# Clearing the sorted rows in sixteen parts behind the first stage's stores, with new engine orders

## The chip, the cores and the metric

The kernel runs on one core of one Trainium2 chip. The metric is the device time in microseconds of one execution, as the median of several runs. Lower is better.

## What is computed

The reference is a decoder of two layers on 64 sequences of 64 tokens of width 128, all in float32. Every sublayer is followed by a residual sum and a layer norm:

```
x = ln(x + retention(x))                 # layer 0: 8 heads, decay mask, group norm, gate
x = ln(x + cross_attention(ctx, x))      # 8 heads, masked, context of width 256
x = ln(x + moe(x))                       # 8 experts, top 2, merged by similarity, rerouted
x = ln(x + attention(x))                 # layer 1: 16 heads of 64, banded, softmax
x = ln(x + cross_attention(x, ctx))      # 16 heads of 8, over context and own tokens
x = ln(x + block(x))                     # attention, then 8 experts of width 512, top 2
```

The last sublayer's experts are sparse in the kernel: each token's row is copied to two places, sorted by expert, in a DRAM tensor `rows_x` of 38,912 rows of 132 floats. Rows of the sorted tensor to which no token goes must be zero, so `rows_x` is cleared before the first row is scattered into it. This clearing is what the change moves.

## The kernel before

**Tiling and stages.** The 64 sequences are 16 groups of 4 (256 tokens). Four slots (buffers and two PSUM banks each) hold four groups at a time, so there are four passes; group `4*n + s` is pass `n` in slot `s`. The program has four stages. Stage one (streams 0 to 15 of the orders, one for each group) does layer 0's sublayers: `first` is the retention, `second` the cross attention and all eight experts (steps `u0` to `u7` for the up products, `d0` to `d7` for the down products). Stage two (streams 16 to 31, for groups 0 to 15) does layer 1 up to the routing and scatters each token's row into `rows_x`. Stage three runs 39 tiles of 256 sorted rows through the wide experts, and stage four adds up and normalises.

**Between stages one and two** stands a small chain (`between`, steps `br`, `br.1`, `br.2` of stream 32): when the gate of all 16 groups is known, VectorE and TensorE work out which experts are merged and from which rows of `y_mid` each token's two results come (`first_rows`). GpSimd then gathers them (`fetch`, L1015).

**Orders.** Each engine is an in-order queue. What it issues next isn't decided at run time: for every stage and engine `ORDERS` holds a list of (stream, count) pairs, and `in_turn` advances the generator of that stream by so many steps. A step is what stands between two `yield`s, and it begins with the semaphore waits of its work. So a step whose input is late holds up everything behind it on that engine. A step is written here as stream:name, as 15:g for the gate of group 15.

**SyncE's queue (SP)** issues the plain DMAs. In stage one a stream's steps are `q` (the next pass's context and mask, four DMAs), `o2` (the next pass's x), `gb` (store of the state `x_mid`), `ye3` (store of four experts' results to `y_mid`), `u7` (the next pass's `XT`, L760) and `ye7` (the other four experts' results). Before this, SP issues the loads of the first pass, the weights `wb`, and then the clearing: it waits for a zeroed SBUF tile `blank` and issues four DMAs (L818), each of a quarter of `rows_x`. Nobody waits for them but GpSimd's first `fetch` of stage two:

```
if n == 0 and s == 0:
    pool.wait_ge(s_clear, 16 * (XROWS // 128 // BLANK))
```

The lines that the steps below touch: L1841 the projections of retention (`qk`, four matmul pairs), L1801 the 64-row scores, L1949 and L1828 an expert's up and down products, L1808 the turning of the state (`x`, `t1` to `t4`), L1938 the gate product of stage one (`g`), L1125 ScalarE's normalisation of the state (`on`), L2166 the gate product of stage two, L2171 the ranks (`rk`), L1707 the places on VectorE, L1081 the scatter into `rows_x`.

Of the kernel before, what the change touches and what calls it, by code (L numbers as in the profile page):

```python
# [30 lines left out]
SLOTS = 4  # L31
# [13 lines left out]
XROWS = 7 * CAP + 40 * NT  # L45
BLANK = XROWS // 128 // 4
# [77 lines left out]
def part_of(stage, i):  # L124
# [4 lines left out]
ORDERS = dict(sp1=(0, 1, 2, 1, 3, 1, 0, 1, 1, 3, 2, 1, 0, 4, 3, 1, 1, 3, 2, 2, 4, 2, 2, 1, 3, 1, 2, 1, 3, 3, 4, 4, 6, 1, 5, 2,  # L129
# [5 lines left out]
    pool1=(0, 4, 1, 2, 2, 2, 3, 2, 0, 1, 1, 2, 2, 1, 1, 1, 2, 1, 3, 2, 2, 1, 0, 2, 3, 1, 1, 2, 2, 2, 4, 2, 3, 1, 4, 2,  # L135
# [292 lines left out]
def build(nc, d, out, groups):  # L428
    passes = groups // SLOTS
    ctx = ExitStack()  # L430
    with ctx:
# [63 lines left out]
        blank = sb("blank", [128, 4 * WIDE])  # L495
# [252 lines left out]
        def _(sp):  # L748
# [26 lines left out]
            def loads(n, s):  # L775
                load_xT(n, s)
                load_context(n, s)
                load_x(n, s)

            def first(n, s):  # L780
                yield from ()

# [145 lines left out]
        def _(pool):  # L928
# [78 lines left out]
            def fetch(n, s):  # L1007
                if n == 0 and s == 0:
                    pool.wait_ge(s_clear, 16 * (XROWS // 128 // BLANK))
# [1300 lines left out]
```

## Time and profile before

| what | us |
|---|---|
| median of 3 runs | 1558.77 (1558.26 to 1558.95) |
| the profiled execution | 1557.2 |
| its span, first to last instruction | 1555.4 |
| TensorE busy in the span | 1366.5 (88%) |
| VectorE, ScalarE, GpSimd busy | 1109.8, 935.6, 671.9 |

The profile is of one execution. The span is 1.8 us under that execution's own time, and the median of the runs is 1.6 us over it. TensorE is the busiest engine. Its busy time is no floor by itself: it counts matmuls at the clock that was granted at the time, and the share differs from stage to stage. Stage one ends at about 480 us, stage two at about 1320, stage three at about 1490.

### The profile page before, as it was taken

What the parts mean: (1) busy time and instruction counts of PE and PEld (TensorE: products, weight loads), DVE (VectorE), ACT (ScalarE), POOL (GpSimd) and SP (SyncE); (2) the same over time, 40 slices, a digit from 0 to 9 for tenths busy, and PEclk for the clock granted to TensorE, in tenths of its full rate; (3) what the DMA queues carried; (4) which work ended last, traced back from release to release, by engine and by line L of the source; (5) the groups of instructions that cost most, each with busy time, mean ns of one, the idle gap of its engine ahead of it and who ended that gap; (6) DMA issues with size and microseconds to landing.
All of it is one profiled execution on the core that took longest, in us unless ns stands there. A gap on an engine that the chain in (4) does not pass through costs nothing.

```text
span 1555.4 us, 47442 instructions
## 1 busy us (share of the span) xinstructions
PE 1366.5 (88%) x19262; PEld 1123.0 (72%) x19262; DVE 1109.8 (71%) x3476; ACT 935.6 (60%) x2469; POOL 671.9 (43%) x1048
## 2 busy tenths in 40 slices
PE   5899999999988998899998899998899984999951
PEld 4688888888876777676776677776777763888851
DVE  3777787887876758888667887778876775445556
ACT  2555665655544687855878658795568962545412
POOL 5514433533316214655234753337441344254455
PEclk8899999999999999999999999999999996999985
DMA  9952122121022000110000110011100003676851
GB/s 333 384 174 83 35 83 92 53 65 66 15 74 74 9 12 18 44 30 29 10 21 25 36 43 10 14 32 37 29 23 9 13 23 100 208 224 211 237 148 42
DMA packets 112155, 123.21 MB, mean 79 GB/s; under 512 B 21984, under 2 KB 85216, under 8 KB 111680
## 3 DMA queue, kind: packets, MB, share of 16 engines
q1 hardware_dynamic: 105344, 106.53, 21.7%
q0 software_dynamic: 6592, 13.64, 2.8%
q8 instruction: 152, 2.49, 0.7%
q14 instruction: 67, 0.55, 0.1%
HBM read 64.99 MB, written 55.15 MB: 77 GB/s over the span
## 4 chain that ended last, share of the span: by engine, by line
PE 48%; DVE 23%; POOL 8%; ACT 8%; issue 6%; DMA 5%; SPq 2%; DVEq 0%; POOLq 0%; ACTq 0%
PE bank L1949 6%; PE bank L1816 5%; PE bank L1801 3%; PE bank L1828 3%; DMA Q<-in_wm 2%; PE bank L2036 2%; PE bank L2071 2%; PE bank L1997 2%; DVE P L1581 2%; DVE gs L1580 2%; ACT P L1226 2%; PE bank L1993 2%; PE bank L2203 2%; PE bank L2196 2%; POOL rows_x L1081 2%
## 5 line engine op out<-in xcount | busy, mean ns | idle before, releaser
L1816 PE MATMUL bank<-const,P 128*128 128x128 f32 x1152 | 167.9, 280 | 9.9 <-ACT P L1226 4.1
L1816 PEld LDWEIGHTS bank<-const,P 128*128 128x128 f32 x1152 | 129.8, 142 | 39.4 <-ACT P L1226 10.0
L1226 ACT ACTIVATE P<-bank,gs 128x128 f32<-128x128 f32 x512 | 141.3, 393 | 26.4 <-DVE gs L1570 25.9
L1949 PE MATMUL bank<-XT,wb 128*128 128x256 f32 x512 | 140.4, 398 | 7.0 <-ACT PT L1131 3.8
L1036 POOL TENSOR_TENSOR P<-P,gs 128x512 f32<-128x512 f32 x64 | 66.5, 1047 | 157.1 <-DVE gs L1617 156.7
L1234 ACT ACTIVATE PT<-bank 128x512 f32<-128x512 f32 x192 | 108.2, 614 | 28.9 <-PE bank L1816 28.6
L1091 POOL DMA_INDIRECT y_rows<-R,gidx x78 | 74.7, 958 | 92.5 <-DVE R L1756 73.7
L1570 DVE TENSOR_REDUCE gs<-bank 128x4 f32<-128x512 f32 x128 | 82.1, 682 | 39.4 <-PE bank L2071 38.8
L1949 PEld LDWEIGHTS bank<-XT,wb 128*128 128x128 f32 x512 | 89.3, 192 | 22.2 <-ACT PT L1131 7.5
L1580 DVE TENSOR_REDUCE gs<-bank 128x8 f32<-128x512 f32 x128 | 87.1, 681 | 24.5 <-PE bank L2009 12.1
L1198 ACT ACTIVATE P<-bank 128x256 f32<-128x256 f32 x128 | 48.5, 380 | 84.5 <-PE bank L1949 83.8
L1327 ACT ACTIVATE PT<-bank,Q 128x256 f32<-128x256 f32 x156 | 64.8, 475 | 56.5 <-PE bank L2196 55.7
L946 POOL TENSOR_SCALAR rstd<-mv 128x2 f32<-128x2 f32 x80 | 18.1, 226 | 183.1 <-DVE mv L1358 182.3
L1219 ACT ACTIVATE P<-P 128x512 f32<-128x512 f32 x128 | 80.3, 643 | 19.7 <-DVE P L1581 19.3
L1581 DVE TENSOR_TENSOR P<-bank,gs 128x512 f32<-128x512 f32 x128 | 88.5, 691 | 4.4
L1081 POOL DMA_INDIRECT rows_x<-XW,places x64 | 64.4, 1006 | 49.4 <-DVE places L1707 39.3
L2196 PE MATMUL bank<-XT,Q 128*128 128x256 f32 x312 | 77.1, 385 | 4.8 <-DMA Q<-in_wm 4.8
L1828 PEld LDWEIGHTS bank<-wb,P 128*128 128x128 f32 x512 | 73.5, 193 | 9.7 <-DVE P L1511 4.6
L1828 PE MATMUL bank<-wb,P 128*128 128x128 f32 x512 | 78.4, 280 | 2.3 <-DVE P L1511 2.2
L1015 POOL DMA_INDIRECT Q<-y_mid,first_rows x64 | 64.3, 1004 | 29.5 <-DVE first_rows L1556 16.6
L2203 PE MATMUL bank<-Q,PT 128*128 128x128 f32 x624 | 76.1, 275 | 0.0
L2203 PEld LDWEIGHTS bank<-Q,PT 128*128 128x128 f32 x624 | 74.8, 192 | 1.5
(298 smaller groups left out, 3723.3 us busy)
## 6 DMA issues: line engine op xcount, KB each, us to landing
Q<-in_wm SPq DMA_DIRECT2D x39, 578.5 KB, 4.2
rows_x<-blank SPq DMA_DIRECT2D x4, 5016.0 KB, 37.7
y_mid<-PT SPq DMA_DIRECT2D x16, 512.0 KB, 3.1
y_mid<-D SPq DMA_DIRECT2D x16, 512.0 KB, 3.0
XW<-rows_x SPq DMA_DIRECT2D x39, 132.0 KB, 2.5
wb<-in_wb SPq DMA_DIRECT2D x1, 4228.0 KB, 15.0
V<-in_ctxT SPq DMA_DIRECT2D x32, 128.0 KB, 3.4
XT<-in_xT SPq DMA_DIRECT2D x16, 128.0 KB, 2.2
```

The source lines that it names most:

```text
L1081: pool.indirect_dma_start(d["rows_x"][:, :], bass.IndirectOffsetOnAxis(ap=places[:, (n * SLOTS + s) * T + t, k:k + 1], axis=0), XW[s][:, t ...
L1219: act.activation(P[s][:, i, :], P[s][:, i, :], ACT.Exp, scale=scale).then_inc(p.of(s), 1)
L1226: ins = act.activation(P[s][:, i, 128 * g:128 * g + 128], banks[s][i][:, 128 * g:128 * g + 128], ACT.Exp, bias=gs[s][:, 0, 4 * i + g:4 * i ...
L1234: act.activation(dst[:, i, :], banks[s][i][:, :], ACT.Copy).then_inc(pT.of(s), 1)
L1570: dve.tensor_reduce(gs[s][:, 0, 4 * i:4 * i + 4], banks[s][i][:, :].rearrange("p (g m) -> p g m", m=128), AX.X, ALU.min).then_inc(b_s_sub. ...
L1580: st2(dve.tensor_reduce(mx, v, AX.X, most))
L1581: dve.tensor_tensor(P[s][:, i, :].rearrange("p (g m) -> p g m", m=width), v, each(mx, width), ALU.subtract).then_inc(s_sub.of(s), 1)
L1816: last = pe.transpose(tile(banks[s][i], t), tile(P[s][:, i, :], t), ident)
L1828: last = mm(tile(half(s, i + 1), t), tile(P4[s][:, i + 1, :], t), tile(B("down"), e), start=True, stop=True)
L1949: mm(half(s, 2 * (e % 2) + k), tile(B("gu"), 2 * e + k), XT[s][:, :], start=True, stop=True).then_inc(a_up_ps.of(s), 1)
L2196: mm(half(s, c), tile(part(wm[s], WM, "w1"), c), XT[s][:, :], start=True, stop=True).then_inc(m_up_ps.of(s), 1)
L2203: ins = mm(tile(half(s, 0), t), tile(PT4[s][:, c, :], t), tile(part(wm[s], WM, "w2"), c), start=c == 0, stop=c == NC - 1)
```

## The change

The four clearing DMAs ahead of the first stage are gone. In their place stands `clear_rows(k)`, which clears 4 or 5 of the 76 blocks of four rows that each partition holds, called once for each group directly behind its `gb` store. The first call waits for `blank`. GpSimd's `fetch` waits for all 16 parts. Nothing else in the code is changed; but the orders of stages one, two and three are written anew for all five queues. Stage four's are the same.

```
-BLANK = XROWS // 128 // 4
...
+            def clear_rows(k):
+                fours = XROWS // 128 // 4
+                lo, hi = fours * k // groups, fours * (k + 1) // groups
+                sp.dma_start(d["rows_x"].rearrange("(p a r) d -> p a (r d)", p=128, r=4)[:, lo:hi, :],
+                             over(blank[:, :], hi - lo)).then_inc(s_clear, 16)
...
                 sp.wait_ge(a_x.of(s), a_x.at(n, s, use=1))
                 sp.dma_start(token_rows(x_mid, n, s), X1[s][:, :, :]).then_inc(stored[s], 16)
+                if n == 0 and s == 0:
+                    sp.wait_ge(s_blank, 1)
+                clear_rows(n * SLOTS + s)
                 yield "ye3"
...
             sp.dma_start(wb[:, :], d["wb"]).then_inc(s_wb, 16)
-            sp.wait_ge(s_blank, 1)
-            each_row = XROWS // 128
-            for at in range(0, each_row, BLANK):
-                sp.dma_start(d["rows_x"].rearrange("(p a r) d -> p a (r d)", p=128, r=4)[:, at // 4:(at + BLANK) // 4, :],
-                             over(blank[:, :], BLANK // 4)).then_inc(s_clear, 16)
...
-                    pool.wait_ge(s_clear, 16 * (XROWS // 128 // BLANK))
+                    pool.wait_ge(s_clear, 16 * groups)
```

How far the orders moved, counted after writing every list out step by step. A step's move is the difference of its positions in the two lists.

```
queue, stage        steps   mean move
SP, one and two       148        1.4
GpSimd, one and two   448        1.2
ScalarE, one and two 1504        0.5
VectorE, one and two 1219        0.3
TensorE, one and two 2146        0.6
SP, three              78        1.4
GpSimd, three          39        1.1
ScalarE, three        195        1.7
VectorE, three         78        1.4
TensorE, three        273        2.4
```

The places of the lists that the prediction speaks of, written out (b before, a after):

```
SP, start      b  0:q 2:q 3:q 0:o2 1:q 1:o2 1:gb 2:o2 0:gb 0:ye3 0:u7 0:ye7 3:o2 1:ye3 1:u7 1:ye7 2:gb 2:ye3 4:q 4:o2 2:u7 3:gb 2:ye7 3:ye3 3:u7
               a  2:q 3:q 0:q 0:o2 0:gb 0:ye3 2:o2 0:u7 0:ye7 1:q 1:o2 1:gb 1:ye3 1:u7 1:ye7 3:o2 2:gb 2:ye3 2:u7 3:gb 4:q 2:ye7 3:ye3 3:u7
SP, end of one b  12:gb 12:ye3 15:gb 12:ye7 13:gb 13:ye3 16:ls 13:ye7 17:ls 14:gb 14:ye3 14:ye7 18:ls 15:ye3 15:ye7 19:ls
               a  12:gb 12:ye3 13:gb 14:gb 14:ye3 15:gb 12:ye7 16:ls 14:ye7 13:ye3 13:ye7 18:ls 17:ls 15:ye3 15:ye7 19:ls
TensorE, start b  0:qk 0:qk.1 0:qk.2 0:qk.3 0:vg 2:qk 0:st 0:y 0:y.1 3:qk 3:qk.1 3:qk.2 3:qk.3 2:qk.1
               a  0:qk 0:qk.1 0:qk.2 0:qk.3 0:vg 1:qk 0:st 1:qk.1 0:y 0:y.1 2:qk 1:qk.2 1:qk.3 3:qk
TensorE, 1->2  b  14:u5.1 14:d4 13:u7.1 14:u6 14:u6.1 14:d5 14:u7 14:u7.1 15:x 14:d6 15:g 15:u0 15:u0.1 15:u1 15:u1.1 13:d6 13:d7 br
               a  14:u5.1 14:d4 13:u7 13:u7.1 15:x 14:u6 14:u6.1 14:d5 15:g 14:u7 14:u7.1 15:u0 15:u0.1 15:u1 15:u1.1 14:d6 14:d7 br
ScalarE, 1->2  b  14:u4 14:d3 14:u5 14:d4 13:u7 14:u6 14:d5 15:on 14:u7 15:x 15:u0 15:g
               a  14:d3 13:u6 13:d5 12:d7 15:on 14:u5 14:d4 13:u7 15:x 14:u6 14:d5 14:u7 15:u0 15:g
TensorE, 2->3  b  30:t4 30:g 30:rk 31:t4 31:g 31:rk
               a  30:t4 30:g 31:t4 30:rk 31:g 31:rk
VectorE, 2->3  b  30:g 30:gb 30:rk 31:g 31:gb 31:rk
               a  30:g 30:gb 31:g 30:rk 31:gb 31:rk
```

## Rows read from the trace of the kernel before

**Rows 1.** Page, section 1: busy time of each engine

```profile
PE 1366.5 (88%) x19262; PEld 1123.0 (72%) x19262; DVE 1109.8 (71%) x3476; ACT 935.6 (60%) x2469; POOL 671.9 (43%) x1048
```

**Rows 2.** Windows: PE, PEld, DVE, ACT, POOL busy, PE clock, DMA share, GB/s

```profile
18.60:64.30 45.70, 36.41 (x525) 29.92 (x524) 29.18 (x72) 19.73 (x50) 29.95 (x35) 0.87 1.03 382
...
88.00:450.00 362.00, 348.77 (x3929) 302.98 (x3928) 286.06 (x892) 214.79 (x571) 134.16 (x206) 1.00 0.20 62
...
700.00:1000.00 300.00, 279.10 (x4886) 218.09 (x4885) 231.05 (x621) 215.12 (x569) 132.34 (x211) 1.00 0.09 24
```

**Rows 3.** Waits of PE on a DMA, 0 to 88 us, then 88 to 450

```profile
PE bank L1841 <- DMA XT<-in_xT: 3.2, 1, 3.2
...
PE bank L1841 <- DMA XT<-in_xT: 2.1, 1, 2.1
```

**Rows 4.** Timeline of SP, 18 to 90 us: start, duration, line, tensors

```profile
18.25 45.99 SPq L818 DMA_DIRECT2D rows_x<-blank  x4
64.34 14.65 SPq L768 DMA_DIRECT2D V<-in_ctxT  x2
...
87.38 0.81 SPq L768 DMA_DIRECT2D V<-in_ctxT  x2
```

**Rows 5.** Page, section 6: the clearing's DMAs, KB each, us to landing

```profile
rows_x<-blank SPq DMA_DIRECT2D x4, 5016.0 KB, 37.7
```

**Rows 6.** L760 of slot 1 at 6.87 us; timeline 16 to 21 us

```profile
DMA to landing us min/median/max: 8.1/8.1/8.1
...
16.70 0.42 DVE L1436 SCALAR_TENSOR_TENSOR Q<-Q,bank 128x256 f32<-128x256 f32 x1 [3.82 <-ACT Q L1152]
...
17.49 1.22 PE L1841 MATMUL bank<-XT,wa 128*128 128x256 f32 x2 [3.23 <-DMA XT<-in_xT]
...
18.64 1.99 PE L1801 MATMUL bank<-D,PT 64*64 64x128 f32 x32
```

**Rows 7.** Timeline of SP and PE, 135 to 151 us

```profile
143.59 0.82 SPq L768 DMA_DIRECT2D V<-in_ctxT  x2
...
146.22 1.47 SPq L760 DMA_DIRECT2D XT<-in_xT  x1
...
135.86 1.99 PE L1949 MATMUL bank<-XT,wb 128*128 128x256 f32 x8
...
150.29 1.62 PE L1841 MATMUL bank<-XT,wa 128*128 128x256 f32 x6 [2.15 <-DMA XT<-in_xT]
```

**Rows 8.** Timeline at the end of stage one, 447 to 465 us

```profile
447.45 0.22 POOL L956 TENSOR_SCALAR shift<-shift 128x2 f32<-128x2 f32 x1
...
450.30 0.86 ACT L1125 ACTIVATE XW<-R,shift,rstd 128x128 f32<-128x128 f32 x2
...
452.33 0.61 PE L1938 MATMUL bank<-wa,XT 128*128 128x8 f32 x4
...
464.31 1.22 POOL L1015 DMA_INDIRECT Q<-y_mid,first_rows  x1 [16.64 <-DVE first_rows L1556]
```

**Rows 9.** Timeline at the end of stage two, 1305 to 1314 us

```profile
1305.32 0.58 PE L2171 MATMUL bank<-gs,const 128*128 128x16 f32 x2 [3.52 <-DVE base L1423]
...
1307.02 0.17 DVE L1707 CAST places<-small 128x4 uint32<-128x4 f32 x1
1307.30 1.02 PE L2166 MATMUL bank<-wb,XT 128*128 128x8 f32 x4 [0.47 <-ACT XT L1213]
...
1309.46 0.33 DVE L1389 TENSOR_TENSOR small<-gs 128x2 f32<-128x2 f32 x1
...
1311.39 0.95 POOL L1081 DMA_INDIRECT rows_x<-XW,places  x1 [0.30 <-issue]
...
1313.79 0.95 POOL L1081 DMA_INDIRECT rows_x<-XW,places  x1 [1.45 <-DVE places L1707]
```

**Rows 10.** Windows, as rows 2, in the first 24 us

```profile
20.00:24.00 4.00, 3.20 (x46) 2.65 (x42) 1.86 (x4) 0.00 (x0) 0.00 (x0) 0.50 1.02 385
```

**Rows 11.** Waits, 1320 to 1490 us: us in total, times, longest

```profile
DVE small L1740 <- DMA Q<-in_wm: 24.5, 13, 6.4
```

More of the change, by code:

```diff
@@ L126, in part_of @@
     return f"{stage}.{i}" if i else stage
-ORDERS = dict(sp1=(0, 1, 2, 1, 3, 1, 0, 1, 1, 3, 2, 1, 0, 4, 3, 1, 1, 3, 2, 2, 4, 2, 2, 1, 3, 1, 2, 1, 3, 3, 4, 4, 6, 1, 5, 2,
[5 rows of a table removed]
-    pool1=(0, 4, 1, 2, 2, 2, 3, 2, 0, 1, 1, 2, 2, 1, 1, 1, 2, 1, 3, 2, 2, 1, 0, 2, 3, 1, 1, 2, 2, 2, 4, 2, 3, 1, 4, 2,
[14 rows of a table removed]
-    act1=(0, 4, 1, 3, 0, 1, 2, 3, 3, 3, 1, 1, 0, 3, 2, 1, 0, 1, 1, 2, 3, 1, 0, 1, 1, 1, 0, 2, 2, 1, 0, 1, 1, 2, 0, 1,
[58 rows of a table removed]
-    dve1=(0, 7, 2, 2, 3, 2, 0, 1, 1, 2, 0, 1, 1, 1, 0, 1, 1, 2, 2, 1, 1, 1, 3, 1, 1, 1, 2, 2, 3, 2, 1, 1, 0, 1, 2, 1,
[52 rows of a table removed]
-    pe1=(0, 5, 2, 1, 0, 3, 3, 4, 2, 4, 1, 4, 3, 1, 1, 1, 0, 2, 1, 3, 2, 1, 3, 1, 0, 1, 2, 2, 3, 1, 0, 1, 1, 2, 0, 1,
[79 rows of a table removed]
-    sp3=(1, 1, 3, 2, 1, 1, 5, 1, 2, 1, 0, 2, 4, 1, 7, 1, 2, 1, 6, 1, 4, 1, 5, 1, 6, 1, 7, 1, 8, 2, 11, 1, 9, 2, 10, 2,
[3 rows of a table removed]
-    pool3=(1, 1, 0, 1, 2, 1, 4, 1, 3, 1, 7, 1, 5, 1, 6, 1, 11, 1, 8, 1, 10, 1, 9, 1, 13, 1, 12, 1, 15, 1, 16, 1, 14,
-         1, 18, 1, 17, 1, 20, 1, 21, 1, 19, 1, 23, 1, 22, 1, 24, 1, 25, 1, 27, 1, 26, 1, 30, 1, 28, 1, 29, 1, 33, 1,
-         31, 1, 32, 1, 34, 1, 35, 1, 36, 1, 37, 1, 38, 1),
-    act3=(0, 1, 1, 1, 2, 1, 0, 4, 3, 1, 1, 4, 2, 3, 5, 1, 2, 1, 3, 4, 4, 3, 6, 1, 4, 2, 5, 4, 7, 1, 6, 2, 7, 1, 6, 2,
[5 rows of a table removed]
-    dve3=(3, 1, 2, 1, 0, 1, 1, 1, 0, 1, 1, 1, 2, 1, 3, 1, 6, 1, 4, 2, 7, 1, 5, 2, 6, 1, 8, 1, 9, 1, 7, 1, 10, 1, 11,
[4 rows of a table removed]
-    pe3=(0, 1, 2, 1, 1, 1, 0, 2, 3, 1, 0, 1, 1, 1, 0, 1, 1, 3, 0, 2, 2, 2, 1, 2, 2, 2, 4, 1, 5, 1, 3, 4, 2, 2, 4, 4,
[9 rows of a table removed]
@@ new lines @@
+ORDERS = dict(sp1=(2, 1, 3, 1, 0, 4, 2, 1, 0, 2, 1, 6, 3, 1, 2, 3, 3, 1, 4, 1, 2, 1, 3, 3, 5, 1, 4, 5, 6, 2, 5, 3, 7, 1, 5, 2,
[5 rows of a table added]
+    pool1=(0, 4, 1, 2, 2, 2, 3, 2, 0, 1, 1, 2, 2, 1, 1, 1, 2, 1, 3, 2, 1, 1, 2, 1, 0, 2, 2, 1, 3, 1, 1, 1, 3, 1, 2, 1,
[15 rows of a table added]
+    act1=(0, 4, 1, 3, 0, 1, 2, 3, 3, 3, 1, 1, 0, 3, 2, 1, 0, 1, 1, 2, 3, 1, 0, 1, 1, 1, 0, 2, 2, 1, 0, 1, 1, 2, 0, 1,
[57 rows of a table added]
+    dve1=(0, 7, 3, 2, 0, 1, 1, 2, 2, 2, 0, 1, 1, 1, 0, 1, 1, 2, 2, 1, 1, 1, 3, 1, 1, 1, 2, 1, 3, 2, 2, 1, 1, 1, 0, 1,
[53 rows of a table added]
+    pe1=(0, 5, 1, 1, 0, 1, 1, 1, 0, 2, 2, 1, 1, 2, 3, 5, 2, 3, 1, 1, 2, 1, 0, 2, 1, 3, 2, 1, 3, 1, 2, 1, 0, 1, 2, 1,
[79 rows of a table added]
+    sp3=(3, 2, 2, 1, 7, 1, 1, 2, 2, 1, 6, 1, 0, 2, 4, 1, 5, 1, 4, 1, 5, 1, 6, 1, 7, 1, 8, 2, 9, 2, 10, 2, 11, 2, 12,
[3 rows of a table added]
+    pool3=(0, 1, 1, 1, 3, 1, 2, 1, 5, 1, 4, 1, 7, 1, 6, 1, 8, 1, 9, 1, 10, 1, 11, 1, 13, 1, 14, 1, 12, 1, 16, 1, 15,
+         1, 17, 1, 18, 1, 21, 1, 19, 1, 20, 1, 24, 1, 22, 1, 23, 1, 27, 1, 26, 1, 25, 1, 28, 1, 30, 1, 29, 1, 31, 1,
+         33, 1, 32, 1, 34, 1, 36, 1, 35, 1, 37, 1, 38, 1),
+    act3=(0, 1, 1, 1, 0, 4, 1, 3, 3, 1, 1, 1, 3, 1, 2, 5, 5, 1, 4, 1, 3, 3, 4, 4, 5, 2, 7, 1, 5, 2, 6, 5, 8, 1, 7, 4,
[5 rows of a table added]
+    dve3=(0, 1, 1, 1, 2, 1, 3, 1, 0, 1, 1, 1, 2, 1, 5, 1, 3, 1, 4, 2, 5, 1, 8, 1, 6, 2, 7, 2, 10, 1, 11, 1, 8, 1, 9,
[3 rows of a table added]
+    pe3=(0, 1, 1, 1, 2, 1, 3, 1, 0, 4, 1, 4, 0, 2, 3, 2, 4, 1, 1, 2, 2, 4, 5, 1, 3, 2, 2, 2, 3, 2, 6, 1, 4, 3, 7, 1,
[9 rows of a table added]
```

458 rows, old and new, of tables (ORDERS, act1, act3, dve1) are left out of this document.

## Prediction

> **What bounds the kernel now.** I read the page first. TensorE is busy for 1366.5 of the span's 1555.4 us [rows 1], so time is won where TensorE stands idle, and lost where it is made to wait. The windows show where that is [rows 2]. While the four clearing DMAs drain, 18.6 to 64.3 us, the DMA engines are full (share 1.03, 382 GB/s) and TensorE is busy for 36.41 of 45.70 us. From 88 to 450 us, the rest of stage one, DMA has a share of 0.20 and TensorE is busy for 348.77 of 362 us: 13.2 us of idle time in all. In stage two a stretch of 300 us has 279.10 busy, so 20.9 idle.
>
> It is tempting to read the full DMA and the idle TensorE of the first 88 us as cause and effect. The list of waits doesn't bear it out: up to 88 us TensorE waits for a DMA once, 3.2 us, and from 88 to 450 us once again, 2.1 us [rows 3]. The first of these ends at 17.49 [rows 6], before the first clearing DMA is issued at 18.25 [rows 4]. The rest of the idle time in the ramp is the latency of four groups going through a chain of small steps on all engines, with no expert products yet to fill the gaps.
>
> What the clearing does hold is SP. Its four issues last 45.99 us, and the first context load behind them another 14.65 [rows 4]. That load is for pass two, which starts after 100 us. So the clearing is nearly free before the change, and taking it away from there wins by itself nearly nothing. What is left is what the new orders do, and whether the parts hurt where they now stand.
>
> **The clearing, removed at the start: 0.** SP is free from 18.7 us instead of from 79. But its next steps wait for their own inputs: the context of slot 3 is issued at 87.38 us, when its buffer falls free [rows 4], long after the clearing's issues. No engine waits for an earlier SP step. Bounds: 0 above; below, the clock rival under "rivals".
>
> **The sixteen parts: 0, at most 10.** The total is the same: 4 x 5016 KB [rows 5] is 20.5 MB, one part 1.28 MB on average, and at 382 GB/s [rows 2] 3.4 us of all DMA engines. The window from 88 to 450 us has 80% of DMA time unused, 290 us, for 16 x 3.4 = 54 us. The issue on SP was 46 us for four because the queue was full; each part goes into a nearly empty one, and an issue there takes 0.4 to 0.5 us as the 0.81 for two loads shows [rows 4]. What a part can cost is to stand ahead of an urgent transfer: those issued behind it land up to 3.4 us later. Urgent are the `XT` loads (u7) and the second y stores (ye7). In the new list no u7 follows another group's gb directly: 0:gb and its part go out at about 91 us, behind 0:o2, and 0:u7 only when its product is done; 2:u7 stands ahead of 3:gb. At the end 15:gb's part stands ahead of 12:ye7, at about 449 us, and lands at about 454; the store behind it is down by 458, and GpSimd's first gather, the only one that asks for both, starts at 464.31 [rows 8]. That cover of 6 us also hides the new wait for all 16 parts. Without it, every us of delay there would be a us of the kernel.
>
> The Trainium skill, "DMA: Bandwidth & Descriptors", section "Queues, rings and completion order", says that each DMA engine consumes the descriptors of one issuing queue in ring order. By that rule the context load issued behind the clearing had to wait for all of it, and the trace agrees. The same rule speaks against the change, as each part is put into SP's only queue in the midst of loads that someone needs; the rival of parts ahead of loads prices it.
>
> **The orders, stage one: three places, -6.0 in all.** Of many moved steps I price those that touch an idle time of TensorE.
>
> *The start, -1.5.* Before, TensorE has 2:qk ahead of 0:st. Slot 2's XT is late, TensorE idles for 3.23 us, runs the 1.22 us product, and starts 0:st at 18.64, although its last input, VectorE's L1436, was there at 16.70 + 0.42 = 17.12 [rows 6]. After, 1:qk stands there. Slot 1's XT was issued at 6.87 and took 8.1 us [rows 6], so it is there at 14.97; 1.22 us later, at 16.2, the product is done, before 17.12. So 0:st starts at about 17.16, 1.48 us earlier. It is on the chain to group 0's experts, the first filler that TensorE gets. Bounds: 0 if other slots' steps hold group 0 up anyway, -1.5 for the value taken.
>
> *The XT load of group 6, -2.1.* Before, SP has 4:q and 4:o2 ahead of 2:u7. 4:q waits for its buffer until 143.59, so the XT load is issued at 146.22 and TensorE waits 2.15 us for it [rows 7]. The product that frees XT ended with the L1949 row at 135.86 + 1.99 = 137.85. After, 2:u7 stands ahead of 3:gb and 4:q, is issued at about 138 and lands at about 142, even behind what is left of 2:gb's part. TensorE asks for it at 148. The wait goes: -2.1. I find none that takes its place: 2:ye7 goes behind 4:q, at about 147 by ScalarE's last copy, no later than before. Bounds: -2.1 and 0.
>
> *The turn to stage two, -2.4.* The chain `between` starts with group 15's gate. Its normalisation is ready for ScalarE at 447.45 + 0.22 = 447.67, but ScalarE has the copies and tanh of groups 13 and 14 ahead of it and gets there at 450.30; the gate product follows at 452.33, and the first gather at 464.31 [rows 8]. After, 15:on stands ahead of 14:u5, 14:d4, 13:u7 and 14:u6, and on TensorE 15:x and 15:g stand ahead of three or four steps that they followed. 15:on can start at 447.7, 2.6 us earlier; TensorE has 15:x behind 13:u7.1, which costs some of it. I take -2.4 for the gate and for all behind it: the rows for the gather, and group 15's own expert chain, which also ends later than anything else in stage one. Bounds: 0 (group 14's products, which now go later, could hold the end) and -2.6, the whole advance on ScalarE.
>
> **The orders, stage two to three: +1.4.** Before, TensorE waits 3.52 us in 30:rk while 31:t4 could run. After, 31:t4 goes first, and 31:g can follow 30:rk at once: 1305.32 + 0.58 and the second product of about 0.4 give 1306.3 in place of 1307.30 [rows 9]. But VectorE now takes 31:g ahead of 30:rk. 31:g starts as L2166 ends and is done at 1309.46 + 0.33 = 1309.79; all one us earlier makes 1308.8, and 30:rk, some 0.9 us, ends at 1309.7 in place of 1307.02 + 0.17 = 1307.19. So group 30's four scatters begin 2.5 us later. They ended before at 1311.39 + 0.95; with the gap of 0.30 the next could start at 1312.64, and group 31's first started at 1313.79 [rows 9]. After, it is 1312.64 + 2.5 = 1315.1: 1.4 us later, and stage three waits for the last scatter. Bounds: 0 and +2.5.
>
> **The rest of stages two and three: 0, give or take 4.** The lists differ nearly everywhere by a step or two. TensorE's idle time there is 7% of a long stretch [rows 2], and in stage three it hangs on when SP issues a tile's weights: VectorE waits 24.5 us for them in 13 times [rows 11]. I see no place where one order is plainly better. The 4 us is chosen: the three places of stage one move 6 us in a stage whose idle time is of the same kind, and they were the larger ones.
>
> **The sum.** -1.5 - 2.1 - 2.4 + 1.4 = -4.6 us. The profiled execution would take 1557.2 - 4.6 = 1552.6 and the median, which stood 1.6 above it, 1554.2 (-0.29%).
>
> **The rivals.**
> *The gains are absorbed (0.24).* In-order queues eat slack: a step that comes early waits behind another. Only the XT wait goes (-2.1) and the end of stage two gives 1.4 back: 1558.1. For it: most moves are small; against: all three places are on what TensorE waited for.
> *The ramp gets faster (0.12).* From 17.4 to about 24 us TensorE is granted half its clock, 1.2 GHz (0.50 [rows 10]), after the idle time that ended at 17.49. If the smaller gap leaves it at 2.4 GHz, the 1.22 + 1.99 us [rows 6] and the 3.20 us busy from 20 to 24 [rows 10] shrink by up to half, 3.2 us: 1551.0. Against: it also dropped later in the ramp, in gaps that stay.
> *Parts ahead of loads, slower (0.08).* If parts meet all twelve XT loads, which then land late by 3.4 us less TensorE's margin of about 2.5, they cost 12 x 0.9 = 10.8: 1565. It decides (slower by over 0.2%) from 0.65 us for each, 7.7 us in all, which just undoes the 4.6 and adds 3.1. Against: the new list keeps the two apart.
> *Stage three's new order is worse (0.08).* 39 tiles, each with weights 0.2 us later, are 7.8 us: 1562.0. It decides at the same 7.7 us. That stage's list moved most, 2.4 steps in the mean.
> *The change doesn't do what it says*: if the parts bunch up, 13:gb, 14:gb and 15:gb at the end (10 us of DMA) and not 3, they could reach past 464 us. They would have to be delayed to after 454; counted with the parts rival.
>
> **How the numbers follow.** The located gains carry through: 0.48, at 1554.2, its own range 1550 to 1558.5. 0.2% of 1558.77 is 3.1 us, about what a measurement of this kernel can tell from no change; so faster is below 1555.7, slower above 1561.9. Faster: 0.38 of the first case, the ramp's 0.12, 0.05 of the absorbed one: 0.55. Slower: 0.12 from the last two and 0.02 elsewhere: 0.14. Same: 0.31. The range reaches from the ramp case with a good draw of the 4 us, 1547.5, to under the slower cases, 1560.5.
>
> **What would show it.** SP: 16 issues of about 0.45 us, landing in 4 to 6 us. The list of waits: no XT wait near 148 us; L1801 first at 17.2 rather than 18.64; the gather L1015 first at 459 to 462 us; stage three's first product no earlier against that than before, by 1 to 2 us. DMA between 18 and 88 us no longer full, and TensorE's idle time there nearly the same. It would be wrong if the first gather comes at 464 or later, if a wait for a DMA appears in stage one, or if the stretches 490 to 1280 and 1320 to 1490 change by more than 4 us.

## Result and profile after

The changed kernel takes 1568.05 us in the median of 4 runs (1566.31 to 1568.92); the kernel before took 1558.51 beside it. The ratio is 1.006, 95% interval 1.0044 to 1.0076: slower by 9.5 us, where 4.6 us faster was predicted. The profiled execution took 1567.24 us, with a span of 1565.2.

Lines of the changed kernel stand 3 higher than before (L1801 is L1804), on SP's queue up to 8. Its page first: section 1, and the clearing's row of section 6.

```profile
PE 1369.9 (88%) x19262; PEld 1121.0 (72%) x19262; DVE 1115.6 (71%) x3476; ACT 932.9 (60%) x2469; POOL 670.2 (43%) x1048
...
rows_x<-blank SPq DMA_DIRECT2D x12, 1320.0 KB, 5.9
rows_x<-blank SPq DMA_DIRECT2D x4, 1056.0 KB, 5.3
```

TensorE's busy time is 3.4 us more than it was [rows 1], in a span that is 9.8 us longer. So 6.4 us of the loss are idle time of TensorE. The parts land in 5 to 6 us, as said. The windows, with columns as in [rows 2], answer to those of before:

```profile
18.60:64.30 45.70, 35.27 (x517) 29.20 (x517) 32.51 (x81) 21.71 (x55) 31.71 (x40) 0.96 0.26 103
88.00:450.00 362.00, 347.21 (x3857) 301.08 (x3856) 286.83 (x906) 212.19 (x572) 130.59 (x200) 1.00 0.35 123
700.00:1000.00 300.00, 275.92 (x4753) 214.66 (x4751) 231.76 (x603) 212.50 (x567) 127.39 (x202) 1.00 0.09 23
```

Up to 450 us all looks as hoped. DMA is no longer full, and the timeline has 0:st (L1804), the XT load of group 6, group 15's normalisation and the first gather early, against 18.64, 146.22, 450.30 and 464.31 [rows 6 to 8]:

```profile
17.27 1.10 PE L1804 MATMUL bank<-D,PT 64*64 64x128 f32 x32 [1.01 <-DVE Q L1439]
...
134.53 0.34 SPq L759 DMA_DIRECT2D XT<-in_xT  x1
...
440.34 0.88 ACT L1128 ACTIVATE XW<-R,shift,rstd 128x128 f32<-128x128 f32 x2 [0.25 <-POOL shift L959]
...
456.35 1.22 POOL L1018 DMA_INDIRECT Q<-y_mid,first_rows  x1 [16.04 <-DVE first_rows L1559]
```

So stage two starts 8.0 us early. It ends 1.65 us early: the last scatter into the sorted rows starts at 1315.92, and at 1317.57 before. Stage four's first load of results is issued at 1497.52, and at 1487.19 before. Stage two lost 6.3 us, stage three another 12.0.

To find the places I cut the timeline at five events on SP and GpSimd that every kernel has: the first gather; SP's context load (`K<-in_ctxT`, step `out1`) of groups 4, 7, 8 and 11, streams 20, 23, 24 and 27; the last scatter; the first `K<-y_rows`. From those rows, in us between their starts:

```
                       first   20:out1 to  24:out1 to  last scatter
                       gather  23:out1     27:out1     to K<-y_rows
before                 464.3   79.5        86.2        169.6
after                  456.4   83.6        90.9        181.6
```

The columns stand for stage one, the second pass, the third pass and stage three. Over 18 more traces (table below) the first three are steady: each moves with its own lists (the gather also with the clearing, where the lists are old) and by 4.4 us at most with anything else. Stage three's column is not so steady. With the old lists it lies between 169.6 and 174.9 on one kind of chip and between 187.2 and 194.5 on another.

### The profile page after: what moved, and what is told of

The parts are those of the page before. It is cut to its first block, busy times and chain, and to the rows that moved or that the text cites. A ratio compares the mean times of both kernels' runs of the same rounds, so it can differ in the third digit from the quotient of the medians.

```text
span 1565.2 us, 47454 instructions
## 1 busy us (share of the span) xinstructions
PE 1369.9 (88%) x19262; PEld 1121.0 (72%) x19262; DVE 1115.6 (71%) x3476; ACT 932.9 (60%) x2469; POOL 670.2 (43%) x1048
## 4 chain that ended last, share of the span: by engine, by line
PE 46%; DVE 23%; POOL 11%; ACT 7%; issue 7%; DMA 4%; SPq 1%; DVEq 0%; POOLq 0%; ACTq 0%
PE bank L1819 5%; PE bank L1952 4%; PE bank L2039 3%; PE bank L1996 2%; PE bank L2074 2%; PE bank L2000 2%; PE bank L1804 2%; PE bank L1831 2%; PE bank L2199 2%; POOL rows_x L1084 2%; DMA Q<-in_wm 2%; PE bank L2206 2%; DVE stats L1357 2%; DVE P L1584 2%; POOL Q L1018 2%
## 5 line engine op out<-in xcount | busy, mean ns | idle before, releaser
L1222 ACT ACTIVATE P<-P 128x512 f32<-128x512 f32 x128 | 80.8, 645 | 21.4 <-DVE P L1584 20.9
```

## Experiments

The lists of each stage can be exchanged apart. "New" is the changed kernel's list, "old" that of before. For stages one and two, which share their lists, the steps of streams 0 to 15 and of 16 to 31 were taken each from one kernel, and interleaved as the changed kernel has them. A quarter of stage two is cut where both lists of an engine have issued the same steps: quarter two is 27% to 54% of each engine's steps, quarter three 54% to 78%.

The runs fell on two kinds of chip, and that has to be known to read them. On some, the kernel before took 1558.2 to 1558.5 us; on others 1646.4 to 1647.5. Ratios are always to the kernel before on the same chip. In the table A is the first kind, B the second; then first gather, second pass, third pass and stage three from each trace, in the columns above.

```
kernel               one  clearing two       three | kind median  ratio  [95%]           | gather 2nd  3rd  three
after                new  parts    new       new   | A 1568.05 1.0060 [1.0044,1.0076] | 456.4 83.6 90.9 181.6
n0_new               new  parts    new       new   | A 1568.22 1.0059 [1.0036,1.0082] | 457.6 86.5 91.1 179.3
n1_new12_old3        new  parts    new       old   | A 1564.62 1.0032 [1.0015,1.0048] | 458.2 83.8 90.8 174.9
n2_new1_old23        new  parts    old       old   | A 1554.00 0.9971 [0.9956,0.9985] | 459.2 79.5 86.6 172.7
n3_new_32tx          new  parts    new       1 step| A 1570.44 1.0061 [1.0038,1.0085] | 459.8 85.5 91.0 176.9
y1_q3_peactsp        new  parts    PE,ACT,SP old   | A 1561.53 1.0012 [0.9994,1.0030] | 457.1 79.8 87.7 172.8
y2_q3_pool           new  parts    GpSimd    old   | A 1559.22 0.9998 [0.9980,1.0016] | 459.6 79.3 91.9 169.7
e1_new_old3          new  parts    new       old   | B 1647.23 1.0001 [0.9981,1.0020] | 458.8 83.6 93.4 191.1
e2_old_new3          old  four     old       new   | B 1645.87 0.9981 [0.9951,1.0010] | 462.9 79.3 88.4 191.0
e3_parts_old_orders  old  parts    old       old   | B 1657.71 1.0064 [1.0037,1.0090] | 475.9 79.5 87.9 190.7
w2_parts_old_orders  old  parts    old       old   | B 1659.52 1.0072 [1.0035,1.0109] | 474.7 79.3 87.9 193.9
e5_new1_old23        new  parts    old       old   | B 1643.05 0.9958 [0.9930,0.9985] | 460.8 79.8 88.4 194.5
w1_oldclear_new1     new  four     old       old   | B 1643.07 0.9974 [0.9947,1.0001] | 457.2 79.5 87.9 193.5
x4_oldclear          new  four     old       old   | B 1644.35 0.9991 [0.9968,1.0014] | 459.6 79.5 87.9 191.2
c2_q2                new  parts    qrt 2 new old   | B 1644.29 0.9996 [0.9971,1.0022] | 457.2 85.0 88.1 187.2
c3_q3                new  parts    qrt 3 new old   | B 1653.94 1.0041 [1.0019,1.0063] | 458.1 79.3 93.2 189.0
x1_q3                new  parts    qrt 3 new old   | B 1652.53 1.0027 [0.9998,1.0055] | 460.8 79.4 93.5 190.8
x2_q3_am1_back       new  parts    qrt 3, 1 step   | B 1649.67 1.0026 [0.9992,1.0059] | 457.5 79.5 92.2 188.0
x3_q14               new  parts    qrt 1,4   old   | B 1643.59 0.9962 [0.9933,0.9991] | 457.2 79.5 87.9 190.5
```

**1. Which stage? (e1, e2, e5; then n0, n1, n2)**

```
-ORDERS sp3, pool3, act3, dve3, pe3 of the changed kernel
+ORDERS sp3, pool3, act3, dve3, pe3 of the kernel before            (e1, n1)
+ and the steps of streams 16 to 31 in the order of before as well  (e5, n2)
 the kernel before, with the changed kernel's five lists of stage three (e2)
```

> The changed kernel, with the five lists of stage three from the kernel before. Theory: of the 9.5 us lost, stage three's new lists lost 12.0 (first product to last scatter of a tile: 164.2 us after against 162.5 before is too coarse a measure, so by the last scatter into the sorted rows, 1315.92 against 1317.57, and the last scatter of results, 1495.16 against 1484.84). So this kernel takes 1568 - 12 = 1556, with the last result scatter at about 1483. Rival: stage three only suffers from what it is handed (which transfers are still under way, in which order the last groups end), and its own lists matter little: 1566 or more.

> The kernel before, its clearing and stages one and two untouched, with the changed kernel's five lists of stage three. Theory that the lists cost 12 us wherever they stand: 1570.5. Rival that stage three suffers only from its surroundings in the changed kernel: 1558 to 1560.

> The changed kernel with its new lists for stage one alone: the steps of streams 16 to 31 stand in the places that the changed kernel's lists have for them but in the order of the kernel before, and stage three's lists are those of before. Theory: stage one's gain of 8.0 us (first gather at 456.35 against 464.31) is carried to the end, and both losses (6.3 us in stage two, 12.0 in stage three) go: 1558.5 - 8 = 1550.5. Rival: the gain of stage one is absorbed in stage two whatever its order, as an earlier start meets the same later waits: 1556 to 1558.

These three ran on a chip of kind B. On kind A, n1 repeats e1, n2 repeats e5, and n0 is the changed kernel itself. The old lists with stage three's new ones (e2) have no run on kind A, and the changed kernel itself has none on kind B.

> The changed kernel itself, unaltered, beside the kernel before on the same chip: the reference for the runs beside it. If the chip is like the one of the first comparison (before at 1558.5): 1568. If it is like the one of the last four runs (before at 1647.5, with TensorE often idle for 'issue'), then by what the others gave there, 1.000 for the mix with the old stage three and 0.998 for the old kernel with the new stage three, 1645 to 1650: ratio 0.998 to 1.002.

> The same as e1_new_old3: the changed kernel with the five lists of stage three from before. On a chip with before at 1558.5, the theory that stage three's new lists lost 12 us gives 1556; the rival that they matter little 1566. On a chip with before at 1647, again a ratio near 1.000.

> The same as e5_new1_old23: new lists for stage one alone. On a chip with before at 1558.5: theory 1550.5 (the 8.0 us of stage one kept, both losses gone); rival, the gain absorbed by stage two: 1556 to 1558. On a chip with before at 1647, again about 0.996.

On the chip of kind A the three steps go one way: 1568.22 with all lists new, 1564.62 with stage three's old (3.6 less; 12 expected), 1554.00 with stage two's old too (10.6 less). The second step is clear of noise (intervals 1.0015 to 1.0048 and 0.9956 to 0.9985). The first alone isn't (1.0036 to 1.0082 and 1.0015 to 1.0048). For it speak n3 below, with stage three's new lists but for one step and 5.8 us over n1, and the last column: 176.9 to 181.6 in the three traces of kind A with new lists, 169.6 to 174.9 in the five with old ones. n2 is 4.2 us faster than the kernel before, ratio 0.9971: the fastest version on kind A. Stage two's lists are the main loss, not stage three's. On kind B e5 is also faster (0.9958), and stage three's lists cost nothing that could be measured (e2 0.9981, and 191.0 in the last column, within what the old lists give there).

**2. The clearing by itself (e3, w2: parts with old lists; w1, x4: four DMAs with new lists)**

```
 the changed kernel's code, all its ORDERS from the kernel before         (e3, w2)
 the kernel before with its four clearing DMAs; stage one's lists new     (w1, x4)
```

> The code of the changed kernel (16 parts, one behind each group's store) with every list of the kernel before. It tells what the clearing's move is worth by itself. My prediction's view, parts and freed start both 0: 1557 to 1560. Rival one, the full DMA engines did hold the ramp (granted clock 0.87 before, 0.96 after in 18.6 to 64.3): up to 5 us faster, 1553 to 1556. Rival two, parts ahead of loads in lists not made for them: 4u7's and later XT loads late, 1561 to 1565.

> The same as e3_parts_old_orders: the 16 parts with every list of before. There the first gather waited for the last part (23.5 us of waiting in all, put down to the clearing's DMA) and came at 475.90, 13.0 us after that of the old kernel with old lists; ratio 1.0064. Theory: with the lists of before, 14:gb stands on SP behind 13:ye7 and 17:ls, so the last parts are issued late, and it costs 8 to 12 us on this chip too: 1566 to 1570. Rival: the cost was due to that chip: 1558 to 1560.

> The kernel before with its four clearing DMAs in place, and new lists for stage one alone (stages two and three in the order of before). Against the same lists with 16 parts (1554.0, ratio 0.9971) it tells what moving the clearing is worth by itself. My prediction's view: nothing, 1554, with the first gather within 1 us of 459.2. Rival, the full DMA engines hold the ramp: TensorE's granted clock in 18.6 to 64.3 was 0.87 before and 0.96 after, its busy time 36.41 and 35.27; then most of the gain goes and this takes 1557 to 1560.

> The same as w1_oldclear_new1: four clearing DMAs ahead of all, new lists for stage one alone. There the first gather came at 457.17, as early as with the 16 parts (459.22 and 460.76). Theory: the clearing's move by itself is worth nothing in either direction once the lists are these, 1554. Rival: full DMA engines cost clock in the ramp, 1557 to 1560.

With old lists the parts do harm. The timeline of SP and GpSimd in e3 (its lines stand 4 higher than after's) shows how:

```profile
456.31 0.47 SPq L786 DMA_DIRECT2D rows_x<-blank  x1
...
458.62 1.29 SPq L786 DMA_DIRECT2D rows_x<-blank  x1
...
466.83 1.59 SPq L786 DMA_DIRECT2D rows_x<-blank  x1
...
475.90 1.22 POOL L1022 DMA_INDIRECT Q<-y_mid,first_rows  x1 [23.51 <-DMA rows_x<-blank]
```

SP's old order has 15:gb ahead of 12:ye7 and 13:gb, and 16:ls, 13:ye7 and 17:ls ahead of 14:gb. So the last three parts are issued between 456 and 467, behind each other and a crowd of stores. The second and third take 8.7 and 8.2 us to land, and the last, issued at 466.83, is there at 475.0. The landing of the three together:

```profile
DMA to landing us min/median/max: 5.1/8.2/8.7
```

The gather waits for them until 475.90 instead of 462.9 (e2). This is my rival "the parts bunch up". The new list prevents it by having 13:gb and 14:gb earlier; in n0 the last part is issued at 442.89. By the Trainium skill, "DMA: Bandwidth & Descriptors", section "Queues, rings and completion order", a DMA engine takes a queue's descriptors in ring order, and the late landing agrees: from 455.9 to 468.5 the DMAs landed in the order of their issue, as far as the trace has their landing.

The wait for the last parts is not all of the 12 to 13 us. From group 15's normalisation (ScalarE's `XW<-R,shift,rstd`) to the gather it is 20.9 us in e3 and w2 and 14.0 in before and e2, so 6.9 belong to it. The other 5 or so are lost before the normalisation, which is ready for ScalarE at 451.2 and 452.4, against 447.7 and 446.3. A part of that is the rival "parts ahead of loads": in e3 two parts go out at 92.94 and 96.13, ahead of the first XT load at 98.71, and TensorE's waits for XT from 88 to 455 us are 5.1 us in two times, against 2.2 in one in e2. The rest was not traced.

With new lists and the four DMAs of before, the first gather comes at 457.2 and 459.6 us, as early as with parts (456.4 to 460.8 over 14 traces). So the gain of stage one is the lists', and moving the clearing is worth nothing there that the traces can show. The ratios of w1 and x4 (0.9974, 0.9991) are a little above those of e5 and x3 (0.9958, 0.9962), but the intervals overlap; a gain of 2 to 5 us from the clearing's move isn't excluded.

**3. Which part of stage two? (c2, c3, x1, x3)**

```
 e5_new1_old23, with the new order in quarter 2 (c2), 3 (c3, x1), 1 and 4 (x3)
```

> As n2_new1_old23 (1554.0), with the new order in the second quarter of stage two's lists (27% to 54% of each engine's steps of streams 16 to 31, cut where both lists have issued the same steps), the old one in the rest of stage two and in stage three. The context loads of n1 (new order) and n2 (old order) part in two places: at 803 to 805 us, where n1 falls back by 5 us, and at 1013 to 1020, by 6. This quarter holds the first. Theory: 1554 + 5 = 1559. Rival: what one quarter loses the next makes up: 1554 to 1555.

> As n2_new1_old23, with the new order in the third quarter of stage two's lists (54% to 78%) alone. It holds the second place, where n1 falls back by 6 us near 1013 to 1020 us. Theory: 1554 + 6 = 1560. Rival: the loss needs the first quarter's order before it: 1554 to 1556.

> The same as c3_q3: new order in the third quarter of stage two's lists, old in the rest of stage two and in stage three, new lists in stage one. Where before takes 1558.2 and the same without the quarter 1554.0: theory 1560 to 1562 (group 27's context load is issued 8 us later in c3_q3 than in e5_new1_old23, 1071 against 1063). Rival, on that kind of chip it costs nothing and the loss is spread over all quarters: 1554 to 1556.

> As n2_new1_old23, with the new order in the first and the last quarter of stage two's lists (0 to 27% and 78 to 100%). In n1 against n2 the context loads and the last scatter move by -2 to -4 us up to 784 us, and by nothing from 1131 to the last scatter. Theory: the first quarter gains 2 and the last changes nothing, 1552, the fastest of all so far. Rival: what the first quarter gains is absorbed at the turn to the second pass, 1554 to 1555; and 30:rk behind 31:g at the end costs the 1.4 us that I predicted, 1555 to 1557.

Quarters one and four do no measurable harm or good (0.9962 beside 0.9958), against the 2 us expected. Quarter two lengthens the second pass to 85.0 us and nothing else, ratio 0.9996; quarter three the third pass to 93.2 and 93.5, ratios 1.0041 and 1.0027. Whether quarter two's loss lasts is not shown by c2 alone. Its interval overlaps those of e5 and x3, and in its trace the last scatter starts at 1382.95, at 1384.48 in e5's. On kind A both losses last: n1's passes are 4.3 and 4.2 us longer than n2's, and its last scatter starts at 1322.25 against 1315.09, 7.2 us later, though its first gather was 1.1 us earlier. The ratios of kind B don't add up either: c2, c3 and x1 lie 0.4%, 0.8% and 0.7% over e5, but e1, with all of stage two's lists new, only 0.4%. With intervals of 0.2 to 0.3% to each side, they say which quarters lose and not how much.

**4. Which step in quarter three? (x2, y1, y2)** In the changed kernel the timeline of that place reads so (GpSimd, VectorE, TensorE):

```profile
997.90 0.42 DVE L1636 COPY K<-bank 128x256 f32<-128x256 f32 x1 [0.91 <-PE bank L2050]
997.98 1.10 POOL L1018 DMA_INDIRECT Q<-y_mid,first_rows  x1 [0.17 <-issue]
998.25 3.33 DVE L1670 TENSOR_SCALAR D<-K,const 128x256 f32<-128x256 f32 x2
999.11 2.05 POOL L1039 TENSOR_TENSOR P<-P,gs 128x512 f32<-128x512 f32 x2
...
1002.06 1.32 PE L1804 MATMUL bank<-D,Q 64*64 64x128 f32 x32 [2.29 <-DVE V L1673]
```

GpSimd runs 27:am1 and 27:am1.1, the two halves of one product, back to back, as its new list has them behind 24:fq.1, 24:fq.3 and the gather 24:ya'. VectorE's two L1670 beside them take 3.33 us. TensorE waits 2.29. One such instruction by itself, over the whole kernel (min/median/max in ns), after and in n2:

```profile
L1670 DVE TENSOR_SCALAR D<-K,const x32: 321/351/3074, 584.8 to 1275.3; 128x256 f32<-128x256 f32 x32
```

```profile
L1670 DVE TENSOR_SCALAR D<-K,const x32: 320/349/1127, 590.3 to 1275.2; 128x256 f32<-128x256 f32 x32
```

The first edit put one step of it back:

```
 GpSimd, quarter 3
-24:co 26:out1 24:fq.1 24:fq.3 24:ya' 27:am1 27:am1.1
+24:co 26:out1 27:am1 24:fq.1 24:fq.3 24:ya' 27:am1.1
```

> As x1_q3, with one GpSimd step put back to where the kernel before has it: 27:am1 (the first half of group 27's mask product in its second attention round) ahead of 24:fq.1, 24:fq.3 and the gather 24:ya'. In n1 (new order) it runs at 1004.12, right behind the gather and not waited for; in n2 (old order) at 994.64. Theory: this step in the queue of others is what delays group 27, TensorE's 2.28 us wait in L1804 at 1007 and the late context load: most of the quarter's loss goes, 1554 to 1557. Rival: TensorE's own order (27:aq0 behind 26:as0, 26:as1 and 25:out1 moved) makes group 27 late anyway, and this kernel takes the time of x1_q3 within 2 us.

It missed: 92.2 us, and the ratio of x1 (1.0026), though the longest L1670 fell from 3.07 us (x1) to 2.08. Then whole queues were exchanged in that quarter:

```
 quarter 3: new order on TensorE, ScalarE and SP, old on VectorE and GpSimd   (y1)
 quarter 3: new order on GpSimd alone                                         (y2)
```

> New lists for stage one; in the third quarter of stage two the new order on TensorE, ScalarE and SP, the old one on VectorE and GpSimd; the rest old. Theory: the loss comes from VectorE and GpSimd, whose steps meet: in n1 VectorE's L1670 took 3.07 us in place of 0.31 while GpSimd ran two mask products back to back (1004.12 to 1006.17), behind a VectorE step (26:cq) that waited 0.91 us, and TensorE waited 2.28 us for the result. With both in the old order the span from group 24's to group 27's context load is 87 to 89 us and the ratio to before 0.996 to 0.998. Rival: TensorE's order does it (26:ao1.2 and 26:ao1.3 ahead of 24:co, 27:ap1 behind 25:co, 26:cq, 24:fv, 26:cv and 24:fs0): 91 to 93 us and 1.001 to 1.004.

> New lists for stage one; in the third quarter of stage two the new order on GpSimd alone, all other lists old. Theory that GpSimd's order is enough by itself to disturb VectorE: 91 us or more between the context loads of groups 24 and 27, and a ratio of 1.000 to 1.003. Rival: GpSimd has slack and its order alone does nothing: 87 to 89 us, 0.996 to 0.998.

The third pass answers as the theory says: 87.7 us in y1, 91.9 in y2. The times answer less well: y2's ratio of 0.9998 is at the lower edge of what the theory said (1.000), and y1's of 1.0012 is what the rival said. VectorE's L1670 takes 1.13 us at most in y2, so the long pass doesn't need the meeting of VectorE and GpSimd. The late GpSimd step is met by TensorE directly there, and through it by ScalarE:

```profile
1001.02 2.05 POOL L1039 TENSOR_TENSOR P<-P,gs 128x512 f32<-128x512 f32 x2
...
1002.13 1.12 PE L1819 MATMUL bank<-const,P 128*128 128x128 f32 x4 [3.33 <-POOL P L1039]
...
1004.99 1.57 ACT L1274 ACTIVATE Q<-bank,const 128x256 f32<-128x256 f32 x4 [4.40 <-PE bank L2050]
```

In n2, with the old order, the first half runs at 994.64 and the second at 1000.94, and no such wait appears:

```profile
994.64 1.04 POOL L1039 TENSOR_TENSOR P<-P,gs 128x512 f32<-128x512 f32 x1
...
1000.94 1.05 POOL L1039 TENSOR_TENSOR P<-P,gs 128x512 f32<-128x512 f32 x1
```

So GpSimd's order alone is enough for the late third pass. y2's ratio (0.9998 against n2's 0.9971 on another chip of kind A, 4.2 us) is about that, though the two intervals just overlap. But y1's time doesn't follow its third pass: 1.0012, with a pass only 1.1 us longer than in n2, and its median is 2.3 us over y2's on the same chip. Its trace is longer by about 1 us in each of several stretches: 124.8 against 123.4 between passes two and three, 104.3 against 103.4 from the last context load to the last scatter. New orders on TensorE, ScalarE and SP cost something too, spread out; or this chip was slower for it. That stays open. No run has the new order on every queue but GpSimd's, so whether VectorE's part is needed isn't known, and neither is which of GpSimd's moves does it. It is open too why x2 didn't help: with the other four queues new, 27:am1 was early (1038.59 in x2, 6.2 us ahead of 27:am1.1) and the pass long all the same.

**5. One place of stage three (n3)** In the trace after, TensorE is idle from 1440.5 to 1444.12 for the rows of tile 30, and is then granted half its clock (0.50, 1.2 GHz) until 1450. SP, VectorE and TensorE, then the windows:

```profile
1437.66 0.22 DVE L1743 SCALAR_TENSOR_TENSOR small<-XW,Q 128x2 f32<-128x2 f32 x1 [1.46 <-DMA Q<-in_wm]
...
1439.73 1.61 SPq L865 DMA_DIRECT2D XW<-rows_x  x2
...
1444.12 0.69 PE L1811 MATMUL bank<-const,XW 128*128 128x128 f32 x2 [3.57 <-DMA XW<-rows_x]
...
1444.00:1450.00 6.00, 5.88 (x23) 5.53 (x24) 0.91 (x3) 0.79 (x3) 0.52 (x1) 0.50 0.66 223
```

SP has 32:tx (the load of tile 32's rows) ahead of 30:tx there, and 32:tx waits for tile 28's step on VectorE.

```
 SP, stage three
-27:tw 28:tw 32:tx 30:tx 30:tw 29:tx 29:tw 31:tx
+27:tw 28:tw 30:tx 30:tw 29:tx 29:tw 32:tx 31:tx
```

> The changed kernel with one step moved: on SP's queue of stage three 32:tx stands behind 29:tw rather than ahead of 30:tx. In the changed kernel 32:tx waits on VectorE for tile 28, whose weights arrive late, and holds 30:tx until 1440.55; TensorE idles 3.57 us for that XW and is then granted half its clock for the next 6 us. Theory: the wait and the slow stretch go, 3.6 + about 3 us: the changed kernel minus 6, 1562 where it takes 1568. Rival: the next late transfer is met instead (weights of 30 and 29), minus 0 to 2: 1566 to 1568.

The rival's time was right: 1570.44, no gain. The trace after already says why. A tile's rows are loaded when VectorE is through with the first step of the tile four before. VectorE's new list has these steps in the order 27, 28, 26, and that of tile 26, for which 30:tx waits, ends with this row:

```profile
1439.89 0.17 DVE L1751 CAST gidx<-small 128x2 uint32<-128x2 f32 x1
```

It ends at 1440.06, and 30:tx is issued at 1440.94, 0.88 us later. 32:tx was issued 0.81 us behind its own release, at 1438.92. So 30:tx left as soon as VectorE allowed it, and 32:tx ahead of it held up next to nothing; that it did so "until 1440.55" was my misreading. In n3 the same three steps of VectorE are late, as tile 27's at their head waits 3.87 us for its weights; tile 26's ends at 1446.97, 30:tx goes out at 1447.77, and TensorE waits again:

```profile
1442.52 0.22 DVE L1743 SCALAR_TENSOR_TENSOR small<-XW,Q 128x2 f32<-128x2 f32 x1 [3.87 <-DMA Q<-in_wm]
...
1447.77 0.39 SPq L865 DMA_DIRECT2D XW<-rows_x  x1
...
1451.33 0.44 PE L1811 MATMUL bank<-const,XW 128*128 128x128 f32 x2 [3.33 <-DMA XW<-rows_x]
```

By these rows it is VectorE's order (tile 26 behind 27 and 28) and the landing of their weights that hold this place up. The old list has tile 28, 26, 27. No run puts VectorE's order back, so this is argued from the traces and not shown.

## Why the prediction was wrong, point by point

**The step that failed** is "the rest of stages two and three: 0, give or take 4", with its sentence that I saw no place where one order is plainly better. By the medians of kind A stage two's new lists cost 10.6 us and stage three's 3.6, together 14.2; more than three times the chosen 4 us. In place of 0 the runs showed this. In stage two the second and third pass are each 4 us longer; for the third GpSimd's new order in quarter three is enough (y2), for the second the step wasn't looked for. In stage three TensorE waits longer for rows, and which move does that stayed open. The argument for the 4 us, that stage one's three places were the larger ones, compared an effect that I had looked for with effects that I had not. Two lists written side by side show moves such as that of 27:am1, from ahead of three others to behind them, but they don't price them: putting that one step back changed little (x2). The prediction priced the moves of stage one's queues only where TensorE already waited in the old trace; a move that makes a new wait, where the old trace shows none, can't be found in that way.

**The clearing removed at the start, 0; the parts, 0:** right with these lists, in the trace (gather 457.2 and 459.6 without, 456.4 to 460.8 with parts). The "bunching" rival was real, and it was the lists that kept it off: with old lists the parts cost 12 to 13 us at the gather (474.7 and 475.9 against 462.9), about 7 by bunching and the rest earlier in the stage. The prediction has the four DMAs of before drain by 64.3 us. That is when SP had issued them; the DMA engines stay full to 88 us:

```profile
64.30:88.00 23.70, 22.37 (x201) 18.83 (x197) 17.77 (x54) 13.47 (x35) 4.85 (x12) 0.81 1.01 361
```

The sum doesn't change by it, as TensorE waits for no DMA there.

**Stage one, -6.0:** near in size, in part by luck. Sixteen traces with the new lists have the first gather at 456.4 to 460.8, in the mean 458.4; two with the old lists and the old clearing at 464.3 and 462.9: -5.2. The trace after, with -8.0, was at the early end. By place: 0:st at 17.27 for 17.16 predicted; the XT load of group 6 at 134.53 for about 138, and no XT wait from 88 to 450 us; group 15's normalisation 10 us ahead of before's rather than 2.6, of which the gather kept 8.

Taken apart over the 16 traces with new lists and the two with old lists and the old clearing, the -5.2 is this. The statistics of group 15 are ready for ScalarE 4.6 us earlier, where the start and the XT load were to give 3.6. ScalarE then takes them up 0.03 us later and not 2.6, which is the whole advance that the prediction named as its bound. But from there to the gather it is 16.0 us in each of the 16 traces, against 14.0 in before and e2. These 2.0 us stood nowhere in the prediction. So the turn gave -0.6 and not -2.4, what lies ahead of it gave 1.0 more than said, and the two errors in part cancel. What costs the 2.0 was not looked for; TensorE's waits for VectorE in `between` (L1965 and L1969 in the trace after) are 1.4 and 1.8 us, and were 0.4 and 1.5.

The median of n2 (-4.2 us) shows that the gain lasts to the end when the later stages keep their order: "the gains are absorbed" fell.

**The ramp's clock:** the rival "the ramp gets faster" came true in the clock, and hardly in the time. The trace after, to be set beside [rows 10]:

```profile
20.00:24.00 4.00, 3.64 (x30) 2.89 (x26) 2.46 (x6) 0.42 (x1) 1.30 (x2) 1.00 1.13 416
```

TensorE is granted its full 2.4 GHz there and not 1.2, and 0:st takes 1.10 us and not 1.99. What it did before is idle 0.96 and 1.01 us, at 15.57 and 17.27, in place of 3.23 at once. All four traces with the old lists of stage one (before, e2, e3, w2) have the granted clock at 0.50 from 20 to 24 us, and so have 2 of the 16 with the new ones (e1, x4); the other 14 have 1.00. The clearing doesn't decide it: w1 has full DMA engines and 1.00, e3 and w2 have neither. But the first gather of e1 and x4 (458.8, 459.6) is only 0.5 and 1.3 us behind the mean of the 14 (458.3), so little of the 3.2 us that the rival counted reaches it. The mean over 18.6 to 64.3 us (0.87 before, 0.96 after, 0.89 in n2 and w1) also holds later stretches of half clock and can't be read for this.

**Stage two to three, +1.4:** not confirmed. From the last context load to the last scatter it is 101.5 us before and 102.3 after, but 103.5 in n1 (new) and 103.4 in n2 (old): 0 within what such a stretch varies.

**Stage three's new order worse:** the rival had the right sign on kind A, at 3.6 us by the medians (n0 to n1, not clear of noise by themselves) and 7 by the traces (169.6 to 174.9 with old lists on kind A, 176.9 to 181.6 with new ones). No run shows its weights issued 0.2 us later in each tile; what the traces show is later rows. TensorE's waits for them from 1330 to the stage's end, before (to 1490) and after (to 1500):

```profile
PE bank L1808 <- DMA XW<-rows_x: 3.3, 5, 1.2
```

```profile
PE bank L1811 <- DMA XW<-rows_x: 9.1, 8, 3.6
```

The same sum in every trace, from 14 us behind the last scatter to the first `K<-y_rows`, is 9.1 to 10.6 us in the three with stage three's new lists (after, n0, e2) and 7.8 in n3, and 2.9 to 6.5 in the sixteen with old ones. On kind B it goes without a loss of time (e2). VectorE's wait for weights doesn't tell the lists apart: 24.5 us before [rows 11], 28.3 after, but on kind A 25.5 to 30.6 in the other four with old lists and 25.0 and 26.4 in the other two with new ones. Which of stage three's moves makes the rows late was not settled; the one tried was not it.

**Signs named in advance:** "if the stretches 490 to 1280 and 1320 to 1490 change by more than 4 us" is what happened (6.3 us in stage two, 12.0 in stage three). The first gather was not late, and the one wait of TensorE for a DMA in stage one of the trace after is the 0.96 us for XT at 15.57, which was 3.23 before.

## What to carry to other kernels

A transfer cut into parts is only as free as the queue position of its last part: here the same 16 parts cost nothing measurable with one set of lists and 12 us at the gather with another. When the order of in-order queues is rewritten, look in the new lists for steps that moved behind something that waits, not in the old trace for waits that go; and exchange lists stage by stage before believing or rejecting any: one stage's gain of 4 to 5 us was hidden under two others' losses. Events that every version has, taken from one trace each, localise such a loss to a pass where the total times of single kernels differ by as much as the effect.

## What the runs showed of the hardware

**VectorE beside GpSimd.** VectorE's 128x256 L1670 takes 0.35 us in the median. Its longest is 3.07 us in all seven traces in which every queue has the new order in quarter three (after, n0, n1, n3, e1, c3, x1), beside a gather's issue (1.10 us) and two 128x512 products (2.05 us) of GpSimd, all back to back; 2.08 us in x2, where one of the two products stands earlier; 1.69 in c2; and 1.13 at most in the eleven others. The Trainium skill, "SBUF — State Buffer", section "Who interferes with whom", says that some VectorE operations and GpSimd's share a port pair, which one of them holds for its whole instruction. It names tensor_scalar, which L1670 is, among those that can enter the modes that use the pair; whether L1670 runs in such a mode no run here shows. The trace agrees in kind: the operation started at 998.25, while GpSimd issued the gather, and ended 2.7 us late at 1001.32, 0.16 us behind GpSimd's second product (1001.16). In the other six of the seven, and in x2 and c2, it is 0.15 or 0.16 us as well.

**Two kinds of chip.** The same kernel takes 1558 us on some chips and 1647 on others. Stage one is the same (first gather 464.3 and 462.9). From 530 to 1280 us a B trace (e2, with before's lists there) has waits that an A trace (before) has not or hardly: VectorE, ScalarE and TensorE for "remote" and "issue", that is, for nothing that the profile shows on the core. First e2, then before:

```profile
DVE gs L1582 <- remote: 19.5, 7, 4.8
...
ACT K L1308 <- remote: 7.0, 1, 7.0
...
PE bank L2011 <- issue: 7.1, 14, 1.2
...
PE bank L2089 <- issue: 6.4, 16, 0.5
```

```profile
PE bank L2009 <- issue: 2.8, 2, 1.7
...
PE bank L2087 <- issue: 0.2, 1, 0.2
```

Between 19:out1 and 20:out1, for instance, B takes 138 to 150 us and A 122 to 125, while 20:out1 to 23:out1, with the old lists, takes 79.3 to 79.8 on both. So the loss sits in certain stretches. Its cause was not looked for.
